# Layer 0 projection and attention: values made once, 78-row packs, first loads inside the projection, 512-wide value products

## The chip, the core and the metric

The program runs on one NeuronCore of a Trainium2 chip. Its engines work side by side: TensorE (PE) multiplies matrices, VectorE (DVE) and ScalarE (ACT) work on elements, GpSimd (POOL) too, and SyncE (SP) issues the transfers (DMAs) between HBM and the on-chip memory SBUF. PE writes to the accumulation memory PSUM. The engines are ordered by semaphores alone. The metric is the device time of one execution, in microseconds, lower is better. The kernel before takes 1454.33 us (median of 3 runs, 1447.15 to 1459.47).

## What is computed

Two transformer layers on 2048 tokens of width 128 (2 batches of 1024), each an attention and a mixture of experts, with a layer norm after each of the four parts. The change touches only the first attention, which has 16 heads of width 8 and scores made of distances instead of a softmax:

```python
qh = (q @ Wq).reshape(Bq, Sq, H, D).transpose(0, 2, 1, 3)
kh = (q @ Wk).reshape(Bq, Sq, H, D).transpose(0, 2, 1, 3)
vh = (q @ Wv).reshape(Bq, Sq, H, D).transpose(0, 2, 1, 3)
q_norm = jnp.sum(qh * qh, axis=-1, keepdims=True)
k_norm = jnp.sum(kh * kh, axis=-1, keepdims=True)
qk = jnp.einsum('bhsd,bhtd->bhst', qh, kh)
dist = jnp.maximum(q_norm - 2.0 * qk + jnp.swapaxes(k_norm, -2, -1), 0.0)
scores = jnp.exp(-gamma[None, :, None, None] * SCALE * dist)
mask = jnp.triu(jnp.ones((Sq, Sq), dtype=bool), k=1)
scores = jnp.where(mask, scores, 0.0)
out = jnp.einsum('bhst,bhtd->bhsd', scores, vh)
out = out.transpose(0, 2, 1, 3).reshape(Bq, Sq, H * D)
return out @ Wo
```

## The kernel before

Everything lies transposed: channels or keys on the partitions, tokens along the free axis. A stage is a block; all engines meet at a barrier at its end. The first blocks are these.

**First loads** (L1989). SP loads X (the input, 1 MB) and four small constants, and the block ends when they have landed.

**Projection** (`project_l0`). SP loads Wq, Wk and Hs. Then, for four groups g of 512 tokens, PE makes the queries and keys (L138, L139), ACT, DVE and POOL split each into three bf16 parts, and PE sums the squares of each head (L149), which are split too. SP stores each part to HBM (L122: three DMAs for the queries, five for the keys; L125 and L126: the norms), ten DMAs to a group. The block ends when all 40 have landed, because the attention reads them back in another order, across the groups.

**Attention** (`attention_l0`). An iteration `it` is one batch and four heads, so there are 8. For each, SP loads a pack into one of two slots: QP and KP hold 72 rows of products of parts (three parts by three parts by eight channels), and rows of norms and ones, so that one bf16 product over the partitions gives the distance. The norm rows stand at 72 and at 96, so the slots have 128 rows, whose upper half is first filled by memsets (L238: DVE fills slot 0, POOL slot 1), and SP waits for them before it loads (`slot_set`). The load is ten DMAs (L254 to L259): eight of the pack, X of the batch again (XB), and the value weights of the four heads, spread to 32 columns a head (WV).

The 1024 by 1024 upper triangle of a head is cut into 5 tiles T (TILES0), four 1024 columns wide and the last 512, so an iteration has 20 steps (T, head). Each step goes PE score products into one of three PSUM buffers `ring` (L318), ACT exp into PR (L389), DVE clamp in place (L415), POOL mask of the diagonal blocks (L291), PE value products into the PSUM buffer OUT (L338). An iteration begins with one step more: the values of its four heads (L308), which pass through `ring` too and are copied by ACT to V (L380). PE's order is fixed in the code: it runs the scores LAG = 2 tiles ahead of the value products, and puts one quarter (256 columns) of the value products of a tile behind each score step (`weigh`). The four heads of a product write 32 output rows each, at partitions 0, 32, 64 and 96. The first `weigh` of an iteration waits until DVE has copied OUT of the iteration before (`copy_out`, L420), which DVE does behind its clamps of T = 1. SP loads the pack of `it` when ACT has read all steps of `it - 2` (`ring_read`), then carries the output of `it - 2` to OC by four DMAs (L267).

After the block, the layer norm of this part begins (L501 to L541), and from there on the program is the same before and after.

Of the kernel before, what the change touches and what calls it, by code (L numbers as in the profile page):

```python
# [28 lines left out]
P = 128  # L29
# [57 lines left out]
def project_l0(nc, X, wq, wk, headsel, QS, KS, QN, KN):  # L87
# [5 lines left out]
    with ExitStack() as ctx:  # L93
# [6 lines left out]
        part = sb("p0_part", [P, 2, NPART, TOK], BF16)  # L100
        nrest = sb("p0_nrest", [2 * ROWS, TOK], F32)
        npart = sb("p0_npart", [2 * ROWS, NPART, TOK], BF16)
        psQ, psK, psN = ([pb(f"p0_{n}{s}") for s in range(2)] for n in ("psQ", "psK", "psN"))
        (loaded, proj_ready, squared, k2_done, norm_ready, part1, rest_done, part2, part3, norm_step, norm3, stored) = (
            sem(f"p0_{n}") for n in ("loaded", "proj_ready", "squared", "k2_done", "norm_ready", "part1", "rest_done",
                                     "part2", "part3", "norm_step", "norm3", "stored"))
# [4 lines left out]
        with nc.Block() as block:  # L111
            @block.sync
            def _(sp):
                sp.dma_start(Wq[:], wq).then_inc(loaded, 16)
                sp.dma_start(Wk[:], wk).then_inc(loaded, 16)
                sp.dma_start(Hs[:], headsel).then_inc(loaded, 16)
                for g in range(NG):
                    for m, (dst, copies) in enumerate(((QS, NPART), (KS, NPART + 2))):
                        for i, written in enumerate((part1, part2, part3)):
                            sp.wait_ge(written, g * 2 + m + 1)  # L120
                            for at in range(i, copies, NPART):
                                sp.dma_start(dst[:, at, :, grp(g)], part[:, m, i, grp(g)]).then_inc(stored, 16)  # L122
                    sp.wait_ge(norm_step, g * 3 + 3)
                    sp.wait_ge(norm3, g + 1)
                    sp.dma_start(QN[:, :, grp(g)], npart[0:H, :, grp(g)]).then_inc(stored, 16)  # L125
                    sp.dma_start(KN[:, :, grp(g)], npart[ROWS:ROWS + H, :, grp(g)]).then_inc(stored, 16)  # L126
                sp.wait_ge(stored, NG * (NPART + NPART + 2 + 2) * 16)

            @block.tensor
            def _(pe):  # L130
                pe.wait_ge(loaded, 48)

                def project(g):
                    if g >= 2:
# [71 lines left out]
def attention_l0(nc, x_dram, wv, gamma, QS, KS, QN, KN, OC, kept, load_ahead):  # L206

    NT = len(TILES0)
    RING, LAG = 3, 2
    STEPS = 1 + NT * HQ  # L210
    LOADS = (3 + 3 + 2 + 2) * 16
    assert STEPS % RING == 0
    with ExitStack() as ctx:
        sb, pb, sem = sbuf(nc, ctx), psum(nc, ctx), Sems(nc, ctx)
        QP = [sb(f"a0_QP{s}", [P, HQ, S], BF16) for s in range(2)]
        KP = [sb(f"a0_KP{s}", [P, HQ, S], BF16) for s in range(2)]
        XB = [sb(f"a0_XB{s}", [P, S], F32) for s in range(2)]
        WV = [sb(f"a0_WV{s}", [P, P], F32) for s in range(2)]
        V = [sb(f"a0_V{s}", [P, S], F32) for s in range(2)]
        PR = [sb(f"a0_PR{T}", [P, HQ, S], F32) for T in range(NT)]  # L220
        OALL = sb("a0_OALL", [P, NIT, S], F32)
        gam, ng, lo, hi = (sb(f"a0_{n}", [P, H], F32) for n in ("gam", "ng", "lo", "hi"))
        ring = [pb(f"a0_ring{r}", S) for r in range(RING)]
        OUT = pb("a0_OUT", S)
        pack_loaded = [sem(f"pack_loaded{s}") for s in range(2)]
        slot_set = [sem(f"slot_set{s}") for s in range(2)]
        gamma_loaded, gamma_ready = sem("gamma_loaded"), sem("gamma_ready")
        ring_filled, ring_read, clamped, masked, pv_done, out_read = (
            sem(n) for n in ("ring_filled", "ring_read", "clamped", "masked", "pv_done", "out_read"))


        def set_slot(eng, nc_eng, s):

            for n, (rows, value) in enumerate(((QP[s][64:96], 0.0), (QP[s][96:P], BF16_ONES),
                                               (KP[s][64:96], BF16_ONES), (KP[s][96:P], 0.0))):
                if n:
# [1870 lines left out]
```

## Time and profile before

| | |
|---|---|
| median of 3 runs | 1454.33 us |
| the profiled execution | 1455.11 us |
| its span on the core | 1453.4 us |
| PE busy | 1298.2 us (89%) |
| DVE busy | 1123.5 us (77%) |
| ACT busy | 908.7 us (63%) |
| POOL busy | 482.4 us (33%) |
| first matmul of the program | at 9.80 us |
| first exp of the attention | at 69.73 us |
| last copy of OUT in the attention | at 261.66 us |

The time of an execution is its span and about 2 us around it. A busy share is an average over all stages, and PE's counts matmuls that overlap, so a stage is read from its own stretch of the trace. In a timeline row the first number is the start, the second the time from the first instruction's start to the last one's end, then come engine, line, operation, what it writes and reads, the number of instructions, and in brackets how long the engine had been idle and what ended that. "SPq" is SP's DMA queue; its time is that of the issue, not of the transfer. f32 products come as two matmuls each.

### The profile page before, as it was taken

To read this page: it belongs to the slowest core of one execution; us is meant where nothing else is said; L and a number is where in the kernel's file an instruction comes from. 1 tells how busy PE (TensorE), PEld (TensorE's weight loads), DVE (VectorE), ACT (ScalarE), POOL (GpSimd) and SP (SyncE) were. 2 spreads that over 40 slices of the span, in tenths; PEclk is the share of its full clock that TensorE was granted. 3 is DMA by queue.
4 is the path that set the end of the run, shared out by engine and by line. 5 is a ranking of instruction groups with operands and counts; after the bars stand their busy time and mean duration, and the time that the engine had idled before them with its cause. 6 is when DMAs were issued, how large, how long until landed. Compare 5 with 4: busy or idle time off the path is not lost. (4 is left out here: it accounts for less than half of the span.)

```text
span 1453.4 us, 23547 instructions
## 1 busy us (share of the span) xinstructions
PE 1298.2 (89%) x7982; PEld 740.8 (51%) x7982; DVE 1123.5 (77%) x1729; ACT 908.7 (63%) x1509; POOL 482.4 (33%) x992
## 2 busy tenths in 40 slices
PE   4189898717999999999979999999999999999998
PEld 1133333415877777777743222232222327877776
DVE  4266767385999999999947888888898836688886
ACT  3188888203555555555534488878888865767774
POOL 4254545102434434434324342244224422121310
PEclk8599999957999999999998899999999998999999
DMA  4523321006566666666334475443442201021200
GB/s 133 132 56 82 81 81 31 7 0 134 132 144 151 153 144 154 149 145 155 81 120 118 103 171 135 125 102 92 109 113 66 60 5 60 28 91 73 87 30 30
DMA packets 72014, 140.46 MB, mean 97 GB/s; under 512 B 13243, under 2 KB 45436, under 8 KB 64988
## 3 DMA queue, kind: packets, MB, share of 16 engines
q1 hardware_dynamic: 70752, 138.01, 38.0%
q8 instruction: 60, 0.98, 0.3%
q10 hardware_dynamic: 1152, 1.05, 0.2%
q14 instruction: 50, 0.41, 0.1%
HBM read 121.42 MB, written 16.29 MB: 95 GB/s over the span
## 5 line engine op out<-in xcount | busy, mean ns | idle before, releaser
L1592 ACT ACTIVATE a_PR<-n1a_C 128x512 f32<-128x512 f32 x576 | 299.7, 602 | 80.6 <-PE n1a_C L1498 80.6
L1607 DVE CUSTOM_DVE_ANT_0 OC_last<-a_mring,a_COR 128x1024 bf16<-128x1024 f32 x256 | 302.7, 1218 | 44.6 <-PE a_mring L1465 44.2
L1435 POOL TENSOR_SCALAR_AFFINE_SELECT a_PR<-a_PR 128x128 f32<-128x128 f32 x512 | 136.6, 299 | 251.4 <-ACT a_PR L1592 250.8
L871 ACT ACTIVATE e_HH<-e_H 128x512 fp32r<-128x512 f32 x184 | 116.5, 633 | 162.5 <-DVE e_H L919 162.5
L1498 PE MATMUL n1a_C<-a_QP,a_KP 74*128 74x512 bf16 (+3 forms) x768 | 177.0, 333 | 6.2 <-ACT a_PR L1592 3.3
L415 DVE TENSOR_SCALAR a_PR<-a_PR,a_lo,a_hi 128x1024 f32<-128x1024 f32 (+1 forms) x160 | 122.2, 775 | 77.6 <-ACT a_PR L389 75.0
L389 ACT ACTIVATE a_PR<-a_ring,a_ng 128x1024 f32<-128x1024 f32 (+1 forms) x160 | 155.1, 1034 | 14.8 <-PE a_ring L318 14.1
L1517 PE MATMUL n1a_C<-a_PR,a_V 128*9 128x512 f32 (+3 forms) x1536 | 152.2, 492 | 0.0
L890 DVE TENSOR_TENSOR e_HL<-e_H,e_HH 128x512 fp32r<-128x512 f32 x138 | 140.7, 1019 | 13.3
L1498 PEld LDWEIGHTS n1a_C<-a_QP,a_KP 74*128 74x128 bf16 x768 | 57.1, 98 | 161.8 <-ACT a_PR L1592 120.4
L813 POOL TENSOR_TENSOR e_HL<-e_H,e_HH 128x512 fp32r<-128x512 f32 x46 | 78.8, 1714 | 182.6 <-ACT e_HH L871 182.6
L1886 DVE TENSOR_TENSOR e_HL<-e_GL,e_HH 128x512 fp32r<-128x512 f32 x144 | 108.6, 758 | 38.0 <-ACT e_HH L1854 34.3
L291 POOL TENSOR_SCALAR_AFFINE_SELECT a_PR<-a_PR 128x128 f32<-128x128 f32 x256 | 98.6, 411 | 111.1 <-DVE a_PR L415 111.1
L1847 ACT ACTIVATE e_GL<-e_psF,e_BF 128x512 f32<-128x512 f32 x144 | 99.3, 690 | 53.6 <-PE e_psF L1805 52.7
L919 DVE TENSOR_TENSOR e_H<-e_T,e_ROUTE 128x512 f32<-128x512 f32 x176 | 122.2, 694 | 1.5
L913 DVE TENSOR_TENSOR e_T<-e_SG,e_psU 128x512 f32<-128x512 f32 x176 | 119.6, 679 | 1.2 <-PE e_psU L829 1.1
L864 ACT ACTIVATE e_SG<-e_psG 128x512 f32<-128x512 f32 x184 | 108.7, 591 | 17.4 <-PE e_psG L829 17.4
L338 PE MATMUL a_OUT<-a_PR,a_V 128*32 128x256 f32 (+1 forms) x1280 | 88.7, 371 | 10.3 <-DVE a_OALL L420 10.3
L318 PE MATMUL a_ring<-a_QP,a_KP 128*128 128x512 bf16 (+3 forms) x384 | 88.0, 331 | 9.1 <-ACT a_PR L389 8.8
L1465 PE MATMUL a_mring<-a_KM,a_QM 32*128 32x512 bf16 (+3 forms) x704 | 79.0, 327 | 5.8 <-DVE a_top L1607 2.2
L827 PE MATMUL e_psG<-e_XH,e_WH 128*128 128x512 f32 x184 | 72.7, 395 | 8.6 <-POOL e_WL L808 8.6
L838 PE MATMUL e_acc<-e_HH,e_WH 128*128 128x512 f32 x184 | 76.5, 416 | 2.5 <-POOL e_HL L813 2.2
(260 smaller groups left out, 2322.2 us busy)
## 6 DMA issues: line engine op xcount, KB each, us to landing
e_ROUTE<-routing SPq DMA_DIRECT2D x24, 704.0 KB
a_QP<-q_parts SPq DMA_DIRECT2D x72, 192.0 KB
e_RAW<-in_w_chunks SPq DMA_DIRECT2D x46, 192.0 KB, 7.4
a_QM<-q_parts SPq DMA_DIRECT2D x64, 128.0 KB, 2.8
e_GATE<-gates SPq DMA_DIRECT2D x8, 1024.0 KB, 4.7
e_ROUTE<-routing SPq DMA_DIRECT2D x8, 640.0 KB
a_KP<-k_parts SPq DMA_DIRECT2D x24, 192.0 KB
e_ROUTE<-routing SPq DMA_DIRECT2D x8, 576.0 KB
```

The source lines that it names most:

```text
L389: nc.scalar.activation(PR[T][:, j, 0:WIDTH0[T]], ring[n % RING][:, 0:WIDTH0[T]], ACT.Exp, scale=ng[:, head]).then_inc(ring_read, 1)
L415: nc.vector.tensor_scalar(p, p, lo[:, head], hi[:, head], ALU.max, ALU.min).then_inc(clamped, 1)
L864: nc.scalar.activation(SG[n % 2][:], psG[n % 2][:], ACT.Silu).then_inc(silu_done, 1)
L871: nc.scalar.activation(HH[n % NH][:], HT[n % NH][:], ACT.Copy).then_inc(high_done, 1)
L890: nc.vector.tensor_tensor(HL[n % NH][:], HT[n % NH][:], HH[n % NH][:].bitcast(F32), ALU.subtract)\
L913: nc.vector.tensor_tensor(T[n % 2][:], SG[n % 2][:], psU[n % 2][:], ALU.mult).then_inc(mul_done, 1)
L919: nc.vector.tensor_tensor(HT[n % NH][:], T[n % 2][:], ROUTE[c % NW][:, grp(g)], ALU.mult).then_inc(h_ready, 1)
L1435: last = nc.gpsimd.affine_select(out=d, in_=d, compare_op=keep, fill=0.0, base=0, pattern=[[step, P]], channel_multiplier=-step)
L1498: last = nc.tensor.matmul(ring[n % NRING][:, a - h % 2 * GW:b - h % 2 * GW], KP[s][:, j, var, kb * P:(kb + 1) * P], QP[s][:, h % 2, j, var ...
L1517: last = nc.tensor.matmul(OUT[j * HP:j * HP + VC, a:b], V[:, b0 + kb, v0:v0 + VC], PR[:, g % NPR, j, a:b], start=(T == 0), stop=(T == NT - ...
L1592: nc.scalar.activation(PR[:, g % NPR, j, :], ring[n % NRING][:], ACT.Exp).then_inc(s_read, 1)
L1607: nc.vector.tensor_tensor_reduce(out=junk[:, i % 2, :], in0=mring[k % 2][:], in1=COR[:, c:c + S], scale=1.0, scalar=-3.0e38, op0=ALU.mult, ...
```

## The change

- The first block is gone. SP issues Wq, the first 512 tokens of X, Wk and Hs at the start of the projection, then the rest of X, the constants, the value weights in their own layout, gamma, and the rows of ones.
- QP and KP have 78 rows: the ones are loaded by four DMAs, the norms stand right behind the 72 rows of products, and the eight memsets are gone. One memset of OUT takes their place, since the value products now write 8 of each 32 rows.
- In the projection SP stores groups 0 and 1 (batch 0), waits for these 20 stores and issues the pack of `it = 0`. The stores of groups 2 and 3 are issued in the attention, behind the pack of `it = 1`. Batch 1's packs wait for them.
- The values of all 16 heads are made once, at the attention's start, by 8 products a batch, from X as it lies in SBUF. An iteration has 20 steps and loads eight DMAs.
- A value product is up to 512 wide, two to a tile, behind the second and the fourth score step. Its output is 8 rows a head.
- OALL holds two iterations in place of eight. From the third on, DVE's copy of OUT waits for the DMAs that read the buffer two iterations before.
- The hardware loops over iterations are written out.

The core of the diff:

```diff
+    def load_ahead(self, sp, wv, gamma, ones):
+
+        sp.dma_start(self.WV[:], wv).then_inc(self.ahead_loaded, 16)
+        sp.dma_start(self.gam[:], gamma.partition_broadcast(P)).then_inc(self.ahead_loaded, 16)
+        for s in range(2):
+            for rows in (self.QP[s][PAIRS + 3:PAIRS + 6], self.KP[s][PAIRS:PAIRS + 3]):
+                sp.dma_start(rows.rearrange("p j t -> p (j t)"), ones[0, 0:HQ * S].partition_broadcast(3)).then_inc(self.ones_loaded, 16)
+    def store_part(self, sp, g, m, i):
+
+        at = slice(g * GW, (g + 1) * GW)
+        dst, copies = ((self.QS, NPART), (self.KS, NPART + 2))[m]
+        for copy in range(i, copies, NPART):
+            sp.dma_start(dst[:, copy, :, at], self.part[:, m, i, at]).then_inc(self.stored[g // 2], 16)
...
@@ project_l0, sync @@
-                sp.dma_start(Wq[:], wq).then_inc(loaded, 16)
-                sp.dma_start(Wk[:], wk).then_inc(loaded, 16)
-                sp.dma_start(Hs[:], headsel).then_inc(loaded, 16)
-                for g in range(NG):
...
-                sp.wait_ge(stored, NG * (NPART + NPART + 2 + 2) * 16)
+                sp.dma_start(Wq[:], a["wq0"]).then_inc(loaded, 16)
+                sp.dma_start(X[:, grp(0)], a["xT"][:, grp(0)]).then_inc(loaded, 16)
+                sp.dma_start(Wk[:], a["wk0"]).then_inc(loaded, 16)
+                sp.dma_start(Hs[:], a["head_sum"]).then_inc(loaded, 16)
+                sp.dma_start(X[:, GW:], a["xT"][:, GW:]).then_inc(rest_loaded, 16)
+                for n, tile in consts.items():
+                    sp.dma_start(tile[:], a[n]).then_inc(consts_loaded, 16)
+                shared.load_ahead(sp, a["wv0"], a["gamma"], a["ones16"])
+                for g in range(2):
...
+                sp.wait_ge(consts_loaded, len(consts) * 16)
+                sp.wait_ge(shared.stored[0], shared.STORES)
+                shared.load(sp, 0)
@@ attention_l0 @@
-    STEPS = 1 + NT * HQ
+    STEPS = NT * HQ
...
+                shared.load(sp, 1)
+                for g in range(2, NG):
+                    for m in range(2):
+                        for i in range(NPART):
+                            shared.store_part(sp, g, m, i)
+                    shared.store_norms(sp, g)
+                load_ahead(sp)
+                for it in range(2, NIT):
+                    sp.wait_ge(ring_read, step(it - 1, 0, 0))
+                    if it == NQUAD:
+                        sp.wait_ge(shared.stored[1], shared.STORES)
+                    shared.load(sp, it)
+                    keep(it - 2)
...
+                def values(b):
+
+                    for kb in range(KB):
+                        at = b * S + kb * P
+                        last = nc.tensor.matmul(ring[b][:, kb * P:(kb + 1) * P], X[:, at:at + P], WV[:], start=True, stop=True)
+                    last.then_inc(ring_filled, 1)
...
-                                rows = slice(j * HP, (j + 1) * HP)
-                                last = nc.tensor.matmul(OUT[rows, a:b], V[s][:, kb * P + j * HP:kb * P + (j + 1) * HP],
-                                                        PR[T][:, j, c0 + a:c0 + b], start=(T == 0 and a % GW == 0),
+                                v0 = (q * HQ + j) * HD
+                                last = nc.tensor.matmul(OUT[j * HP:j * HP + HD, a:e], V[:, b * KB + kb, v0:v0 + HD],
+                                                        PR[T][:, j, c0 + a:c0 + e], start=(T == 0), stop=(T == NT - 1),
...
+                            half = {1: 0, 3: 1}.get(j) if T else {2: 0, 3: 1}.get(j)
+                            if half is not None and half <= (WIDTH0[T] - 1) // GW:
+                                weigh(it, T, half)
@@ attention_l0, vector @@
+                    if it >= 2:
+                        dve.wait_ge(kept[it % 2], it // 2 * HQ * 16)
+                    nc.vector.tensor_copy(OALL[:, it % 2, :], OUT[:]).then_inc(out_read, 1)
```

Two places of the order. First PE in iteration 0, from the last two steps of T = 2 to the first of T = 3, where the scores run ahead into iteration 1 (slots 0 and 1 are the last digits of QP and KP). Before:

```order
L318 MATMUL a0_ring1<-a0_QP0,a0_KP0 128x512 [waits ring_read]
L338 MATMUL a0_OUT<-a0_PR2,a0_V0 32x256 x4
L318 MATMUL a0_ring2<-a0_QP0,a0_KP0 128x512 [waits ring_read]
L338 MATMUL a0_OUT<-a0_PR2,a0_V0 32x256 x4
L308 MATMUL a0_ring0<-a0_WV1,a0_XB1 128x128 [waits ring_read,pack_loaded1]
L308 MATMUL a0_ring0<-a0_WV1,a0_XB1 128x128 x7
L318 MATMUL a0_ring1<-a0_QP1,a0_KP1 128x512 [waits ring_read]
L318 MATMUL a0_ring1<-a0_QP1,a0_KP1 128x512
L338 MATMUL a0_OUT<-a0_PR3,a0_V0 32x256 [waits masked]
L338 MATMUL a0_OUT<-a0_PR3,a0_V0 32x256 x3
```

After, the same place:

```order
L345 MATMUL a0_ring2<-a0_QP0,a0_KP0 128x512 [waits ring_read]
L345 MATMUL a0_ring0<-a0_QP0,a0_KP0 128x512 [waits ring_read]
L364 MATMUL a0_OUT<-a0_PR2,a0_V 8x256 x8
L345 MATMUL a0_ring1<-a0_QP1,a0_KP1 128x512 [waits ring_read,pack_loaded1]
L345 MATMUL a0_ring1<-a0_QP1,a0_KP1 128x512
L345 MATMUL a0_ring2<-a0_QP1,a0_KP1 128x512 [waits ring_read]
L345 MATMUL a0_ring2<-a0_QP1,a0_KP1 128x512
L364 MATMUL a0_OUT<-a0_PR3,a0_V 8x512 [waits masked]
L364 MATMUL a0_OUT<-a0_PR3,a0_V 8x512 x3
```

The values (L308) are gone from between the iterations, and two score steps stand together where one value product stood between them.

Second, SP from its last stores of the projection's block to the pack of `it = 0`. Before:

```order
L125 DMA q0_norm_parts<-p0_npart 48x1x512 [waits p0_norm3,p0_norm_step]
L126 DMA k0_norm_parts<-p0_npart 48x1x512
L111 UNCONDITIONAL_BRANCH [waits p0_stored]
L242 UNCONDITIONAL_BRANCH [waits barrier_Pool_Activation_PE_DVE_SP_release]
L244 DMA a0_gam<-in_gamma 128x16
L565 DMA WOT0<-in_wo0 128x128
L254 DMA a0_QP0<-q0_parts 24x4x1024 [waits slot_set0]
L255 DMA a0_KP0<-k0_parts 24x4x1024
```

After, from the last stores of group 1 to the pack of `it = 1`; the stores of groups 2 and 3 follow it:

```order
L124 DMA k0_norm_parts<-p0_npart 48x1x512
L133 DMA a0_QP0<-q0_parts 24x4x1024 [waits p0_stored0,p0_consts_loaded]
L134 DMA a0_KP0<-k0_parts 24x4x1024
...
L136 DMA a0_KP0<-k0_norm_parts 3x4x1024
L164 UNCONDITIONAL_BRANCH
L289 UNCONDITIONAL_BRANCH [waits barrier_Pool_Activation_PE_DVE_SP_release]
L133 DMA a0_QP1<-q0_parts 24x4x1024
```

The first pack now stands ahead of the block's end and behind 20 stores; before it stood behind 40 stores, the barrier and the memsets.

## Rows read from the trace of the kernel before

**Rows 1.** Windows: length, PE, PEld, DVE, ACT, POOL busy (count), PEclk, DMA share, GB/s.

```profile
165.88:189.92 24.04, 21.78 (x225) 8.85 (x224) 16.33 (x21) 20.33 (x23) 12.23 (x32) 1.00 0.31 82
103.00:105.00 2.00, 2.00 (x18) 0.58 (x9) 1.60 (x3) 0.39 (x1) 1.72 (x4) 0.50 0.24 33
105.00:107.00 2.00, 2.00 (x21) 0.78 (x19) 0.45 (x1) 1.11 (x1) 0.73 (x3) 0.69 0.26 41
```

**Rows 2.** Timeline of ACT in iteration 4, and its first exp of the stage.

```profile
69.73 17.80 ACT L389 ACTIVATE a_PR<-a_ring,a_ng 128x1024 f32<-128x1024 f32 x18
...
177.98 1.11 ACT L389 ACTIVATE a_PR<-a_ring,a_ng 128x1024 f32<-128x1024 f32 x1 [0.82 <-PE a_ring L318]
179.59 5.73 ACT L389 ACTIVATE a_PR<-a_ring,a_ng 128x1024 f32<-128x1024 f32 x6 [0.50 <-PE a_ring L318]
...
189.00 1.02 ACT L380 ACTIVATE a_V<-a_ring 128x1024 f32<-128x1024 f32 x1 [1.89 <-PE a_ring L308]
```

**Rows 3.** Timeline of PE in the same iteration.

```profile
162.78 2.05 PE L308 MATMUL a_ring<-a_WV,a_XB 128*128 128x128 f32 x16
164.66 0.59 PE L318 MATMUL a_ring<-a_QP,a_KP 128*128 128x512 bf16 x2
...
171.31 1.48 PE L318 MATMUL a_ring<-a_QP,a_KP 128*128 128x512 bf16 x9
...
176.26 1.07 PE L338 MATMUL a_OUT<-a_PR,a_V 128*32 128x256 f32 x16 [1.46 <-DVE a_OALL L420]
...
177.81 1.07 PE L338 MATMUL a_OUT<-a_PR,a_V 128*32 128x256 f32 x16
178.81 0.61 PE L318 MATMUL a_ring<-a_QP,a_KP 128*128 128x512 bf16 x3
179.35 0.64 PE L338 MATMUL a_OUT<-a_PR,a_V 128*32 128x256 f32 x8
179.92 0.61 PE L318 MATMUL a_ring<-a_QP,a_KP 128*128 128x512 bf16 x3
```

**Rows 4.** Timeline of PE in the second layer's attention, whose value products are 512 wide.

```profile
941.68 1.05 PE L1517 MATMUL n1a_C<-a_PR,a_V 128*9 128x512 f32 x8
942.66 0.82 PE L1498 MATMUL n1a_C<-a_QP,a_KP 74*128 74x512 bf16 x3
```

**Rows 5.** Timeline of SP's queue to the first pack.

```profile
0.82 0.39 SPq L1992 DMA_DIRECT2D X<-in_xT  x1
...
7.88 0.42 SPq L116 DMA_DIRECT2D p_Hs<-in_head_sum  x1
...
27.63 0.59 SPq L126 DMA_DIRECT2D k_norm_parts<-p_npart  x1
...
40.61 0.59 SPq L126 DMA_DIRECT2D k_norm_parts<-p_npart  x1
43.17 0.33 SPq L244 DMA_DIRECT2D a_gam<-in_gamma  x1
...
52.21 0.93 SPq L254 DMA_DIRECT2D a_QP<-q_parts  x1
...
57.73 0.28 SPq L257 DMA_DIRECT2D a_KP<-k_norm_parts  x1
```

**Rows 6.** DMA issues: times, KB each, median us from issue to landing.

```profile
X<-in_xT SPq DMA_DIRECT2D x1, 1024.0 KB, 4.8
```

**Rows 7.** Timeline of PE, POOL and DVE at the stages' borders.

```profile
9.80 2.07 PE L138 MATMUL p_psQ<-X,p_Wq 128*128 128x512 f32 x2 [9.80 <-DMA p_Hs<-in_head_sum]
...
32.23 1.14 POOL L188 TENSOR_TENSOR p_npart<-p_nrest,p_npart 64x512 bf16<-64x512 f32 x1 [0.36 <-DVE p_npart L178]
...
64.93 3.78 PE L308 MATMUL a_ring<-a_WV,a_XB 128*128 128x128 f32 x16 [34.93 <-DMA a_WV<-in_wv]
68.50 1.12 PE L318 MATMUL a_ring<-a_QP,a_KP 128*128 128x512 bf16 x4
...
261.66 1.23 DVE L420 COPY a_OALL<-a_OUT 128x1024 f32<-128x1024 f32 x1 [1.86 <-PE a_OUT L338]
```

More of the change, by code:

```diff
@@ L227, in attention_l0 @@
[L227 to L236, printed above, removed]
-                    eng.wait_ge(slot_set[s], n)
-                nc_eng.memset(rows.bitcast(F32), value).then_inc(slot_set[s], 1)
-            eng.wait_ge(slot_set[s], 4)
+        gamma_ready, out_clear, ring_filled, ring_read, clamped, masked, pv_done, out_read = (
+            sem(n) for n in ("gamma_ready", "out_clear", "ring_filled", "ring_read", "clamped", "masked", "pv_done", "out_read"))
@@ L346, in pair @@
+                    if half == (WIDTH0[T] - 1) // GW:
+                        last.then_inc(pv_done, 1)
+                pe.wait_ge(shared.ahead_loaded, 32)
+                for b in range(B):
+                    values(b)
+                pe.wait_ge(shared.ones_loaded, 64)
+                for T in range(LAG):
+                    for j in range(HQ):
+                        scores(0, T, j)
+                pe.wait_ge(out_clear, 1)
+                for it in range(NIT):
                     for T in range(NT):
-                        ahead = T + LAG < NT or not last_pair
@@ L348, in pair @@
-                        if T + LAG == NT and ahead:
-                            values(it + 1, k + s, 1 - s)
                         for j in range(HQ):
                             if T + LAG < NT:
-                                scores(it, T + LAG, j, s)
-                            elif ahead:
-                                scores(it + 1, T + LAG - NT, j, 1 - s)
-                            for quarter in {0: (), 1: (), 2: (0, 1), 3: (2, 3)}[j] if T == 0 else (j,):
-                                if quarter <= (WIDTH0[T] - 1) // (GW // 2):
-                                    weigh(it, T, s, quarter)
@@ L360, in _ @@
[L360 to L370 removed]
+                                scores(it, T + LAG, j)
+                            elif it + 1 < NIT:
+                                scores(it + 1, T + LAG - NT, j)
@@ L392, in _ @@
-                pair(0, 0, 0, True)
-                pair(1, 1, 1, False)
-                with act.Fori(1, NIT // 2) as k:
-                    for s in range(2):
-                        pair(k * 2 + s, (k % 2) * 2 + s, s, False)
+                            n, head = step(it, T, j), it % NQUAD * HQ + j
+                            act.wait_ge(ring_filled, n + 1)
+                            if j == 0 and it:
+                                act.wait_ge(pv_done, (it - 1) * NT + T + 1)
+                            nc.scalar.activation(PR[T][:, j, 0:WIDTH0[T]], ring[n % RING][:, 0:WIDTH0[T]],
+                                                 ACT.Exp, scale=ng[:, head:head + 1]).then_inc(ring_read, 1)
```

237 lines of the change are left out of this document (95 added, 142 removed).

## Prediction

> **What bounds the kernel now.** I read the timelines of SP, PE and ACT from the start to the end of the first attention, and windows of one iteration. The stages behind it are not touched, so every microsecond by which that attention ends earlier is one off the total.
>
> Up to the first score product everything waits for SP and for transfers. The program's first matmul starts at 9.80, when Hs has landed [rows 7], though SP was free to load it from 0.82 on. SP issues the last of the projection's 40 stores at 40.61 and the next block begins at 43.17 [rows 5], while the projection's last computation ended at 33.37 [rows 7]. The memsets hold the first pack load back to 52.21 [rows 5]. PE starts the values at 64.93, the scores at 68.50 [rows 7], ACT its exps at 69.73 [rows 2].
>
> In the steady iterations PE sets the pace. A period is 24.04, of which PE works 21.78 and ACT 20.33 [rows 1]. PE's 2.26 idle are 1.46 for DVE's copy of OUT [rows 3] and two short waits for `ring`. ACT waits 0.82 and 0.50 behind that same copy, and 1.89 for the values [rows 2]. DVE (16.33) and POOL (12.23) [rows 1] have slack. The last copy of OUT ends at 262.89 [rows 7].
>
> **The start.** (a) First matmul. SP's issues are about 0.45 apart, so Hs, now fourth, is issued at about 2.2. Before it took 1.92 from issue to the matmul [rows 5, 7], giving 4.1. Ahead of it stands a quarter of X; all of X took 4.8 to land [rows 6], so the quarter adds some tenths. I take 4.5, a gain of 5.3 (bounds 4 and 6). The other three quarters of X, issued at 2.7, should land by about 7.5; the second group's projection wants them 3.6 after the first matmul.
>
> (b) Stores. From the first matmul to the issue of group 1's last store were 17.83 (9.80 to 27.63) [rows 5, 7]. SP now has 11 more loads to issue first, 5 us, over at about 8.3; the stores of group 0 then still wait for POOL's third part, so I add nothing. That issue stands at 22.3. A last store's issue to the next block took 2.56 (40.61 to 43.17) [rows 5], landing and barrier, of which some 2.2 are landing. The first pack's issue starts at 24.6 where it started at 52.21. Its eight issues take 5.8 (52.21 to past 57.73) [rows 5], so the block ends at 30.8. The computation of groups 2 and 3 does not hold it: it ended at 33.37 [rows 7] and moves up by 5.3, to 28.1. The remaining 20 stores, with 0.65 each (12.98 for twenty, 27.63 to 40.61 [rows 5]), go behind the pack of iteration 1; batch 1's packs are not wanted for another 60 us, and the pack of iteration 1 itself is issued from 31 on and wanted near 52.
>
> (c) Values and first exp. PE begins at 31. Sixteen value instructions took 3.57 at the start (64.93 to 68.50) [rows 7] and 1.88 in the loop (162.78 to 164.66) [rows 3]. Two batches are 32. With the clock up after the first batch that is 5.5, wholly slow 7.1; I take 5.5. The first pack, 8 to 9 us after 24.6, is there by then. ACT copies the second batch's values (1.02 [rows 2]) and starts its exps at about 37.6. Before: 69.73 [rows 2]. The start gains **32.1** (bounds 28 and 34). DVE's memset of OUT lies under the values; without that cover it would cost about as much as a copy, 1.2.
>
> **The period.** (d) Values gone: 1.88 of PE. (e) Fewer alternations. Two 256-wide quarters in a row take 1.00 (177.81 to 178.81), one between scores 0.57 (179.35 to 179.92) [rows 3]: a quarter streams in 0.43 and each change of kind costs 0.14. A score step between products takes 0.54 (178.81 to 179.35), three in a row 1.48 or 0.47 each [rows 3], so 0.07 more. An iteration loses seven alternations (two in T = 1, 2 and 3, one in T = 4; T = 0 keeps its two): 7 x 0.21 = 1.5. The 512-wide product with few output rows is in this trace: eight instructions of 128x512 with 9 columns go in 0.98 (941.68 to 942.66), beside scores of 74 rows [rows 4], what 2 x 0.43 + 0.14 gives. So neither 8 output rows nor 78 rows cost or gain anything. The Trainium skill (TensorEngine Tiling, Key Properties) says that changing the tiling mode drains TensorE. It states no price; the 0.21 is the trace's.
>
> PE's work becomes 21.78 - 1.88 - 1.5 = 18.4. ACT's is 16 exps at 0.99 (18 in 17.80 [rows 2]) and four half-wide ones at 0.6 by my estimate (0.5 to 0.7, half the width at somewhat over half the time), 18.2. The two engines are now level, and the copy of OUT stays where it is: DVE copies it behind the clamps of T = 1, PE's first value product waits behind three score steps. PE alone gives 18.4 + 1.46 = 19.9, ACT with its 0.82 and 0.50 19.5. As both run through three buffers with products in lumps of 0.98, and ACT outruns PE in the half-wide tile, they add some waits. Laying the steps out one behind the other from one copy to the next, with the durations above, I get 20.4 to 20.8. I take **20.6**, a gain of 3.44.
>
> (f) Seven periods lie between the first exps of iterations 0 and 7: 24.1. In the last there are no scores ahead to interleave; its tail shrinks by about 0.6. Together **24.7** (19.9 would give 29.6, 21.8 only 16).
>
> (g) The rest: OALL's new wait needs DMAs issued more than an iteration earlier; if they were late DVE would stall, with PE behind it and ACT behind PE. A pack load is released at the end of an iteration and wanted some 20 us on, and needs 9. The written-out loops I cost at nothing: iterations 0 and 1 were written out before.
>
> **Sum.** 32.1 + 24.7 = 56.8. The profiled execution took 1455.11 with a span of 1453.4; it becomes 1398.3. It stands 0.8 above the median, so the median is 1397.5; I say **1398**.
>
> **Rivals.**
> 1. *ACT paces.* A lone exp takes 1.11 [rows 2], not 0.99. If they do not close up, ACT needs 16 x 1.11 + 2.8 + 1.3 = 21.9 a period, a gain of 2.1 in place of 3.44: 1398 + 7 x 1.3 = 1407. For it: PE no longer leaves it behind. Against: 18 in a row at 0.99.
> 2. *The clock falls at the copies.* From 103 to 107 the granted clock was 0.50 and then 0.69, right after PE had waited for a copy [rows 1]. That costs 1.0 + 0.6 us. It happened in one of seven copies, and it is in the time before. PE will idle 11% of a period in place of 9%. If it came at every copy: 6 more x 1.6, 1398 + 10 = 1408. The Trainium skill (TensorE: Matmul & The Clock Gate, A second HAM failure mode) says that frequent short idling between groups makes the clock swing. By that rule this rival comes true; the trace so far agrees once in seven.
> 3. *The start does not come forward.* If the pack load still waits for something that I take as free (20 more requests early on, X arriving late), up to 8 us of the 32 stay: 1406.
> 4. *Smoother.* The copy's wait is all that is left, period 19.9: 1393.
> 5. *Slower than before.* If the four products with 8 output rows did not run side by side in the array, a half tile would stream four times 0.86: 2.6 more for each of 9 products, 23 us a period, 1398 + 184 = 1582. It decides from 57 us over 72 products on, that is if one takes more than 1.8 in place of 0.98. Against it stands the 0.98 of [rows 4] with 9 columns.
> 6. *No change*: would need the packs to be read later than computed by 57 us; I see no path.
>
> **How the numbers follow.** My forecast (1388 to 1403) has 0.54, rival 1 0.12, rival 2 0.12, rival 3 0.08, rival 4 with a start at its better bound 0.1, slower 0.02, no change 0.02. The range reaches from rival 4 with one microsecond more at the start and in the tail each (1390, rounded out to 1386) to rivals 1 and 2 with some microseconds of (a) to (c) on top (1414). This kernel's measurement can tell about 1% from no change, that is 1440; all cases but the last two lie below: faster 0.96.
>
> **What would show it.** In the changed kernel: first matmul near 4.5; first pack issue near 24.6, barrier near 31, first exp near 37.6; half-tile products 0.98 to 1.0 apart from what follows; period between first exps 20.4 to 20.8; the copy of OUT still waited for by 1.5; granted clock 1.00 in the iterations; everything behind the attention as long as before. I am wrong if the first exp comes after 43, if the period is above 21.5, or if a later stage has grown.

## The result and the profile after

The changed kernel takes **1404.14 us** (median of 3 runs, 1402.02 to 1405.89) where the kernel before takes 1454.33: a ratio of 0.9685, with the interval 0.9643 to 0.9726. It is faster by 50.2 us. The forecast was 1398, the range 1386 to 1414. So the number was right, but two of its parts were off, and they partly cancel: the gain of the iterations and the stages behind. The experiments are about the first.

| | before | after |
|---|---|---|
| the profiled execution | 1455.11 | 1402.02 |
| its span | 1453.4 | 1400.3 |
| first matmul | 9.80 | 4.78 |
| first pack issued | 52.21 | 24.86 |
| first exp | 69.73 | 38.48 |
| seven periods, from the first exp of iteration 0 to that of iteration 7 | 168.27 | 154.76 |
| last copy of OUT begins | 261.66 | 217.24 |
| layer norm's first instruction on ACT | 266.31 | 221.88 |
| span behind that | 1187.1 | 1178.4 |

Busy times by the page: PE 1279.3 us (91%), DVE 1114.2 (80%), ACT 898.5 (64%), POOL 481.3 (34%).

**The start.** SP's queue and PE after, the places of [rows 5] and [rows 7]:

```profile
22.63 0.59 SPq L124 DMA_DIRECT2D k_norm_parts<-p_npart  x1
24.86 0.89 SPq L133 DMA_DIRECT2D a_QP<-q_parts  x1
...
30.31 0.28 SPq L136 DMA_DIRECT2D a_KP<-k_norm_parts  x1
31.12 0.77 SPq L133 DMA_DIRECT2D a_QP<-q_parts  x1
```

```profile
4.78 2.07 PE L198 MATMUL p_psQ<-X,p_Wq 128*128 128x512 f32 x2 [4.78 <-DMA p_Hs<-in_head_sum]
...
31.17 6.35 PE L333 MATMUL a_ring<-a_WV,X 128*128 128x128 f32 x32 [6.18 <-PEq L164]
```

The last store of group 1 is issued at 22.63, the pack 2.2 behind it, and the eight issues of the pack end just before the next block begins. PE then makes all values in 6.2 us, and ACT can start:

```profile
38.48 11.15 ACT L402 ACTIVATE a_PR<-a_ring,a_ng 128x1024 f32<-128x1024 f32 x11
```

**The iterations.** Windows of the first five of them, each from the first exp of one iteration to that of the next; columns as in [rows 1], the last but two is the granted clock.

```profile
38.48:58.87 20.39, 18.19 (x111) 4.88 (x112) 14.93 (x20) 18.72 (x21) 13.20 (x31) 0.83 0.44 121
58.87:79.22 20.35, 18.09 (x145) 5.28 (x144) 16.03 (x22) 18.74 (x21) 13.20 (x33) 1.00 0.25 68
79.22:101.87 22.65, 20.59 (x145) 5.40 (x144) 15.90 (x22) 18.73 (x20) 13.20 (x33) 0.85 0.23 62
101.87:125.14 23.27, 21.01 (x145) 5.58 (x144) 15.91 (x22) 18.91 (x21) 12.83 (x33) 0.85 0.22 59
125.14:147.06 21.92, 19.66 (x145) 5.35 (x144) 15.90 (x22) 18.73 (x20) 13.19 (x33) 0.92 0.24 63
```

The second is the iteration that the prediction worked out (period 20.35, PE busy 18.09, clock 1.00). Those behind it have the same 145 matmuls and the same work on ACT, but PE is busy for 1.6 to 2.9 us longer, and the granted clock is 0.85 to 0.92. The first, iteration 0, has fewer matmuls and no copy to wait for, and its clock is 0.83; the run with 128 rows below shows what that costs. The seven periods are 20.39, 20.35, 22.65, 23.27, 21.92, 22.86 and 23.32.

Inside such an iteration, windows of 2 us (same columns):

```profile
87.00:89.00 2.00, 0.82 (x4) 0.21 (x3) 1.80 (x3) 2.00 (x3) 1.85 (x5) 0.67 0.02 4
89.00:91.00 2.00, 1.51 (x8) 0.15 (x8) 2.00 (x4) 1.37 (x2) 0.87 (x2) 0.50 0.10 14
91.00:93.00 2.00, 2.00 (x11) 0.41 (x11) 0.51 (x1) 0.61 (x1) 1.64 (x5) 0.50 0.33 49
93.00:95.00 2.00, 2.00 (x13) 0.44 (x6) 0.81 (x1) 0.56 (x2) 0.54 (x2) 0.62 0.01 2
95.00:97.00 2.00, 2.00 (x17) 0.63 (x15) 0.81 (x1) 2.00 (x3) 0.03 (x1) 1.00 0.00 0
```

PE works for 0.82 of the first 2 us (it waits for ring buffers and then for the copy of OUT), the clock goes to 0.50, which is the lower of its two levels, 1.2 GHz, and PE then works without a pause at that level until about 94.5, before 2.4 GHz are granted again. The timeline of PE shows it at the first product behind each copy. First the copy without a fall, then two with:

```profile
69.14 1.04 PE L364 MATMUL a_OUT<-a_PR,a_V 128*8 128x512 f32 x8 [1.47 <-DVE a_OALL L420]
70.12 0.61 PE L345 MATMUL a_ring<-a_QP,a_KP 78*128 78x512 bf16 x3
...
89.48 1.90 PE L364 MATMUL a_OUT<-a_PR,a_V 128*8 128x512 f32 x8 [1.27 <-DVE a_OALL L420]
...
112.14 1.90 PE L364 MATMUL a_OUT<-a_PR,a_V 128*8 128x512 f32 x8 [1.47 <-DVE a_OALL L420]
113.97 1.03 PE L345 MATMUL a_ring<-a_QP,a_KP 78*128 78x512 bf16 x3
114.94 1.90 PE L364 MATMUL a_OUT<-a_PR,a_V 128*8 128x512 f32 x8
```

The wait is about the same 1.46 as before [rows 3] (1.27 at 89.48); the instructions behind it take 1.8 times as long. Six of the seven copies that PE waits for look like the later ones. ACT, which now has little slack, stands behind PE each time:

```profile
115.05 1.11 ACT L402 ACTIVATE a_PR<-a_ring,a_ng 128x1024 f32<-128x1024 f32 x1 [2.02 <-PE a_ring L345]
117.84 2.12 ACT L402 ACTIVATE a_PR<-a_ring,a_ng 128x1024 f32<-128x1024 f32 x2 [1.68 <-PE a_ring L345]
```

**The end of the stage**, DVE's last copy and ACT's first instruction of the layer norm:

```profile
217.24 1.23 DVE L420 COPY a_OALL<-a_OUT 128x1024 f32<-128x1024 f32 x1 [1.96 <-PE a_OUT L364]
```

```profile
221.88 1.28 ACT L513 ACT_TABLE_LOAD   x1 [7.17 <-PEq L288]
```

The last copy comes 44.4 us earlier than before: 31.25 from the start, 13.5 from the seven periods, 0.3 given back behind them. The two profiled executions differ by 53.1; the missing 8.7 lie in stages whose code is the same.

### The profile page after: what moved, and what is told of

It is laid out like the page before. It is cut to its first block and busy times, and to the rows that moved or that the text cites. A ratio compares the mean times of both kernels' runs of the same rounds, so it can differ in the third digit from the quotient of the medians.

```text
span 1400.3 us, 21389 instructions
## 1 busy us (share of the span) xinstructions
PE 1279.3 (91%) x7374; PEld 711.9 (51%) x7374; DVE 1114.2 (80%) x1726; ACT 898.5 (64%) x1503; POOL 481.3 (34%) x988
## 5 line engine op out<-in xcount | busy, mean ns | idle before, releaser
L1432 POOL TENSOR_SCALAR_AFFINE_SELECT a_PR<-a_PR 128x128 f32<-128x128 f32 x512 | 136.2, 296 | 250.2 <-ACT a_PR L1589 249.7
L402 ACT ACTIVATE a_PR<-a_ring,a_ng 128x1024 f32<-128x1024 f32 (+1 forms) x160 | 150.2, 1045 | 26.0 <-PE a_ring L345 26.0
L427 DVE TENSOR_SCALAR a_PR<-a_PR,a_lo,a_hi 128x1024 f32<-128x1024 f32 (+1 forms) x160 | 119.2, 763 | 56.1 <-ACT a_PR L402 55.6
L887 DVE TENSOR_TENSOR e_HL<-e_H,e_HH 128x512 fp32r<-128x512 f32 x138 | 139.4, 1010 | 13.5 <-DVE e_H L904 0.5
L323 POOL TENSOR_SCALAR_AFFINE_SELECT a_PR<-a_PR 128x128 f32<-128x128 f32 x256 | 105.3, 444 | 82.0 <-DVE a_PR L427 82.0
L861 ACT ACTIVATE e_SG<-e_psG 128x512 f32<-128x512 f32 x184 | 108.7, 591 | 23.3 <-PE e_psG L826 23.1
L364 PE MATMUL a_OUT<-a_PR,a_V 128*8 128x512 f32 (+3 forms) x768 | 84.8, 542 | 10.1 <-DVE a_OALL L420 10.1
L345 PE MATMUL a_ring<-a_QP,a_KP 78*128 78x512 bf16 (+3 forms) x384 | 86.1, 351 | 7.8 <-ACT a_PR L402 7.5
```

Of the source, the lines that this page charges most:

```text
L402: nc.scalar.activation(PR[T][:, j, 0:WIDTH0[T]], ring[n % RING][:, 0:WIDTH0[T]], ACT.Exp, scale=ng[:, head:head + 1]).then_inc(ring_read, 1)
L427: nc.vector.tensor_scalar(p, p, lo[:, head:head + 1], hi[:, head:head + 1], ALU.max, ALU.min).then_inc(clamped, 1)
L887: nc.vector.tensor_tensor(HL[n % NH][:], HT[n % NH][:], HH[n % NH][:].bitcast(F32), ALU.subtract)\
L1432: last = nc.gpsimd.affine_select(out=d, in_=d, compare_op=keep, fill=0.0, base=0, pattern=[[step, P]], channel_multiplier=-step)
```

## The experiments

Three theories of why the periods gain 13.5 in place of 24.1:

- **The wait.** PE's wait for DVE's copy is what brings the clock down. Without it there is no fall at these places.
- **The thin operands.** The wait was there before, with one fall in seven copies [rows 1, 3]. What is new are packs of 78 rows and outputs of 8 rows a head, and one or both of them make the difference.
- **The missing values.** The 1.88 us of value products between the iterations are gone, so PE works less between two waits.

"Falls" below counts, of the seven copies for which PE waits, those behind which the first value product takes 1.3 to 2 us instead of 1.04 to 1.07. "Stage end" is the start of ACT's table load. The fall in iteration 0, where PE waits for no copy, is not among the seven.

The first four runs come from one chip, the next four from a second, the last four from a third. The kernel before took 1451.75, 1450.29 and 1452.39 there (medians), so one or two microseconds between runs of different chips say nothing.

**The changed kernel again**, nothing edited.

> The changed kernel as it is, for the spread. Attention as in its first profile: first exp near 38.5, undisturbed periods 20.4, five or six copies of OUT followed by a fall of the granted clock, last copy of OUT near 218. The stages behind the attention were 8.7 us shorter than before in the first pair of profiles although their code is the same. If that is chance, they differ by some microseconds from profile to profile here, and the median lies at 1402 to 1408.

Measured: 1407.96 (ratio 0.9705, 0.9661 to 0.9749). Falls 7 of 7, seven periods 159.15, stage end 228.09. Each copy reads like this one:

```profile
92.44 1.90 PE L364 MATMUL a_OUT<-a_PR,a_V 128*8 128x512 f32 x8 [1.46 <-DVE a_OALL L420]
```

So the falls belong to the kernel, and how many there are, and what one costs, differs between executions: this profile lost 4.4 us more over the seven periods than the first, and its longest period was 24.96, 4.6 above the undisturbed 20.35.

**The copy one tile earlier**, in the changed kernel. OUT is complete soon after T = 0 of the next iteration has been clamped, so DVE can copy it there.

```diff
-                        if T == 1 and it:
+                        if T == 0 and it:
                             copy_out(it - 1)
```

> One line of the changed kernel: DVE copies OUT behind its clamps of T = 0 instead of T = 1. Theory A (PE's wait for the copy brings the clock down): the wait of 1.46 is gone, the granted clock stays 1.00, period 18.9 in all iterations, last copy near 196, total 22 us below the changed kernel, about 1382. Theory B (the clock falls because the new products fill less of the array, wait or no wait): periods 20.5 to 21.5 with falls in most iterations, total 8 to 12 below, about 1393.

Measured: **1383.07** (1374.22 to 1388.35), ratio 0.9521 (0.946 to 0.9582). No fall at the seven places, stage end 201.83. Window of one iteration, then PE and DVE at the copy:

```profile
116.91:136.27 19.36, 18.13 (x145) 5.28 (x144) 16.04 (x22) 18.59 (x20) 14.26 (x33) 1.00 0.28 72
```

```profile
102.88 1.23 DVE L420 COPY a_OALL<-a_OUT 128x1024 f32<-128x1024 f32 x1 [0.36 <-PE a_OUT L364]
```

```profile
105.74 0.61 PE L345 MATMUL a_ring<-a_QP,a_KP 78*128 78x512 bf16 x3 [0.40 <-ACT a_PR L402]
106.28 1.05 PE L364 MATMUL a_OUT<-a_PR,a_V 128*8 128x512 f32 x8
```

The copy is over at 104.1, two microseconds before PE wants OUT, and the product behind it has no wait and its full speed. PE still has its two waits of 0.40 for a ring buffer, and here they bring no fall. The undisturbed period falls by 1.0 (20.35 to 19.36; 18.9 was expected), not by the whole 1.46, and the falls at the copies are gone: together 26.3 us by the stage's end against the run above, 24.9 by the medians. The theory of the wait holds for these falls. The one in iteration 0 is still there (clock 0.83, period 20.34). The run does not say yet why the kernel before got away with the same wait.

**The same line in the kernel before.**

```diff
-                        if T == 1 and not first:
+                        if T == 0 and not first:
```

> The kernel before with the same one line. Both theories: the wait of 1.46 goes, period 24.04 to 22.5; seven times 1.5 and the one fall of 1.7, total 12 below before, about 1442.

Measured: 1442.45 (ratio 0.9933, 0.991 to 0.9957), near the expected 1442, though against the 1451.75 of its chip it gained 9.3 where 12 were expected; period 23.19 where 24.04 stood [rows 1] and 22.5 was expected, stage end 257.94, 8.4 earlier. The wait was worth 9.3 us there and 24.9 in the changed kernel. The difference is what the change made of the wait.

**Quarters again**: value products 256 wide, one quarter behind each score step, the rest as changed.

```diff
...
-                            half = {1: 0, 3: 1}.get(j) if T else {2: 0, 3: 1}.get(j)
-                            if half is not None and half <= (WIDTH0[T] - 1) // GW:
-                                weigh(it, T, half)
+                            for quarter in {0: (), 1: (), 2: (0, 1), 3: (2, 3)}[j] if T == 0 else (j,):
+                                if quarter <= (WIDTH0[T] - 1) // (GW // 2):
+                                    weigh(it, T, quarter)
```

> The changed kernel with value products 256 wide, one quarter behind each score step, as before. The alternations return: PE's work rises by 1.5, an undisturbed period is 21.6 to 21.9. Theory A in its form that PE's idle share matters: fewer falls, since PE idles less; all periods near 21.7, total within 3 us of the changed kernel. Theory B: the falls stay, periods 23 to 24, total 8 above it, about 1412.

Measured: 1402.19 (ratio 0.9658, 0.9601 to 0.9715). Periods from 21.36 to 23.35, five of them at 23.3; stage end 226.87. So falls come with the narrow products too. While the clock falls, undoing the wide products costs nothing that the times show (1402.19 beside 1407.96 and 1404.14). The one period with the clock at 1.00 is 21.77, 1.42 above the 20.35 with the halves, while a fall costs about 1.55 here and 1.6 to 4.6 there. A later run prices the width without falls.

**32 output rows**: the value products take 32 columns of V (8 of the head and the 24 behind them), packs as changed. V gets 24 columns of zeros at its end, and OUT needs no memset.

```diff
-        V = sb("a0_V", [P, B * KB, P], F32)
+        V = sb("a0_V", [P, B * KB, P + HP - HD], F32)
...
-                                last = nc.tensor.matmul(OUT[j * HP:j * HP + HD, a:e], V[:, b * KB + kb, v0:v0 + HD],
+                                last = nc.tensor.matmul(OUT[j * HP:(j + 1) * HP, a:e], V[:, b * KB + kb, v0:v0 + HP],
```

> The changed kernel with value products of 32 output rows a head, as before (24 of them hold products nobody reads). Three theories on why the granted clock now falls at six of seven copies and fell at one before. C (8 output rows): falls become rare here, periods 20.4, total 10 to 13 below the changed kernel, about 1396. R (78 rows in the scores) and V (PE has 3.4 us less work from copy to copy while the wait is as long): nothing changes here, 1405 to 1409.

Measured: 1396.64 (ratio 0.9634, 0.959 to 0.9678). Falls 4 of 7, stage end 220.40. A product takes 1.06 without a fall, 1.04 with 8 rows. The profiled execution took 1392.15, two others 1401.13 and 1402.01; its stage ended only 1.5 before that of the changed kernel's first profile, and its later stages were the shortest of all profiles. The interval of its ratio overlaps those of the two runs of the changed kernel. So this run does not show that the thin outputs bring falls.

**128 rows in the packs**: rows 64 to 127 of the four slots are zeroed by POOL at the projection's start, ones and packs are loaded over them as changed, and 50 rows stay zero. The sum over the partitions is the same.

```diff
-        self.QP = [sb(f"a0_QP{s}", [PAIRS + 6, HQ, S], BF16) for s in range(2)]
-        self.KP = [sb(f"a0_KP{s}", [PAIRS + 6, HQ, S], BF16) for s in range(2)]
+        self.QP = [sb(f"a0_QP{s}", [P, HQ, S], BF16) for s in range(2)]
+        self.KP = [sb(f"a0_KP{s}", [P, HQ, S], BF16) for s in range(2)]
...
+        sp.wait_ge(self.rows_zero, 4)
...
+                for n, t in enumerate(shared.QP + shared.KP):
+                    if n:
+                        pool.wait_ge(shared.rows_zero, n)
+                    nc.gpsimd.memset(t[64:P].bitcast(F32), 0.0).then_inc(shared.rows_zero, 1)
```

> The changed kernel with packs of 128 rows, the 50 others zero (four memsets on POOL at the start, the ones loaded behind them, which may cost the start up to 2 us). Theory R: falls become rare, periods 20.4, total 8 to 12 below the changed kernel. Theories C and V: nothing changes but the start, 1406 to 1411.

Measured: 1391.19 (ratio 0.9583, 0.9553 to 0.9612). First exp at 38.41, as changed. Falls 1 of 7, stage end 207.62. Two iterations, with and without the fall:

```profile
87.83:109.47 21.64, 19.00 (x142) 5.37 (x145) 15.91 (x22) 18.74 (x21) 13.20 (x32) 0.93 0.25 64
109.47:129.81 20.34, 17.77 (x142) 5.27 (x145) 16.02 (x22) 18.74 (x21) 13.20 (x32) 1.00 0.26 68
```

```profile
109.47 1.04 PE L371 MATMUL a_OUT<-a_PR,a_V 128*8 128x512 f32 x8 [1.46 <-DVE a_OALL L427]
```

The wait is there with its full 1.46, and in six of seven copies the clock stays up. Zero rows that add nothing to the result save 13 to 17 us. In iteration 0 the clock stays up too:

```profile
38.41:57.22 18.81, 15.25 (x109) 4.69 (x112) 14.78 (x20) 18.49 (x21) 13.93 (x31) 1.00 0.51 140
```

That is 1.6 us less than the 20.39 of the changed kernel. Until the clock falls, PE does the same in both: from 40 to 42 it is busy for 1.20 of 2 us, in front of each score step it waits 0.40 for a ring buffer, and no copy is involved. Every profile of this case repeats the difference. The nine of kernels with 78-row packs show a granted clock of 0.77 to 0.84 in iteration 0, the five with 128 rows 1.00. Of all that was tried this speaks most plainly for the packs.

**The values once more**: the changed kernel with a 21st step in each iteration, in which PE makes its batch's values again and ACT copies them to a buffer that nothing reads.

```diff
...
+                    for kb in range(KB):
+                        at = b * S + kb * P
+                        last = nc.tensor.matmul(ring[n % RING][:, kb * P:(kb + 1) * P], X[:, at:at + P], WV[:], start=True, stop=True)
...
+                    nc.scalar.activation(VX[:], ring[n % RING][:], ACT.Copy).then_inc(ring_read, 1)
```

> The changed kernel which beside all else makes a batch's values once more per iteration, as one more step of the ring, and never reads them. That prices the values: 1.88 of PE, 1.02 of ACT and its wait, undisturbed period 22.6 to 23.2 for 20.4. Theory V: PE works as long between the copies as the kernel before nearly did, falls become rare, first exp of iteration 0 to that of iteration 7 takes 160, total near 1408. Theories C and R: falls stay, period 24.5 to 25.5, that stretch takes 172, total near 1422.

Measured: 1424.77 (ratio 0.9814, 0.9787 to 0.984). Falls 7 of 7, seven periods 171.0, stage end 242.13. PE's added work does not keep the clock up: the third theory falls. The run also prices the values: 11.9 us over seven periods beside the changed kernel's repetition, which also fell seven times, that is 1.7 a period, close to the 1.88 of step (d). The falls were shorter in this profile, though: periods with a clock of 0.92 to 0.93 took 21.93 there and 24.29 here, 2.4 apart. So the price lies between 1.7 and 2.4, ACT's copy and the ring step included.

**All 40 stores ahead of the first pack**, with the early copy, so that no fall blurs it.

```diff
-                for g in range(2):
+                for g in range(NG):
...
```

> The early-copy kernel (so that no fall of the clock blurs it) with all 40 stores ahead of the first pack. Prices the split of the stores: twenty issues at 0.65 are 13.0 us, first pack issue from 24.9 to 37.9, first exp from 38.5 to 50 or 51 (the pack's landing, under cover of the values so far, may add up to 3), total 12 to 15 above the early-copy kernel, 1395 to 1398. If the start hung on something else, less than 5.

Measured: 1396.05 (ratio 0.9623, 0.9601 to 0.9644), 13.0 above the early copy alone, or 14.4 if each is taken from the kernel before on its own chip. First pack and first exp are 11.6 and 10.9 later, stage end 213.45 (+11.6):

```profile
36.56 0.89 SPq L133 DMA_DIRECT2D a_QP<-q_parts  x1
```

So splitting the stores is worth 11 to 14 us. This profile also has one more fall: in iteration 5 (period 20.40 for 19.36, clock 0.92) behind two waits of 0.40, with the copy long done:

```profile
154.07 0.61 PE L340 MATMUL a_ring<-a_QP,a_KP 78*128 78x512 bf16 x3 [0.40 <-ACT a_PR L397]
155.07 0.61 PE L340 MATMUL a_ring<-a_QP,a_KP 78*128 78x512 bf16 x3 [0.40 <-ACT a_PR L397]
155.61 1.80 PE L359 MATMUL a_OUT<-a_PR,a_V 128*8 128x512 f32 x8
```

So the earlier copy makes falls rare with 78-row packs, and doesn't exclude them.

**Early copy and quarters.** The edit for the quarters is the one above.

> The early-copy kernel with value products 256 wide, one behind each score step. Prices the 512-wide products where no clock fall blurs them. By the sum of the prediction they save 1.4 to 1.5 of PE an iteration: period from 19.36 to 20.2 to 20.8, last copy 7 to 10 later, total 7 to 10 above the early-copy kernel. If the width is worth nothing even there (ACT paces at 19.36): under 2 above it.

Measured: 1395.51 (ratio 0.9622, 0.956 to 0.9684). No fall after iteration 0:

```profile
101.51:122.43 20.92, 19.57 (x212) 6.20 (x210) 15.95 (x22) 19.42 (x20) 14.10 (x32) 1.00 0.25 67
```

PE is busy for 19.57 beside 18.13 with the halves, the period is 20.92 beside 19.36. The 512-wide products are worth 1.56 a period where no fall blurs it, 11.0 by the stage's end (212.82 for 201.83) and 12.4 in all; 7 to 10 were expected.

**Early copy and 128 rows.**

> The early-copy kernel with packs of 128 rows, 50 of them zero. If a fall needs both, the wait for the copy and the thin packs, there is nothing left to save: period 19.36, total within 3 us of the early-copy kernel (1380 to 1386). If the thin packs cost something beside the falls, 4 or more below it.

Measured: 1383.3 (ratio 0.9511, 0.944 to 0.9583), period 19.39, stage end 201.34: the same as the early copy with 78 rows, as far as the times show. Thin packs stream neither faster nor slower. They cost through the clock, and with the early copy that is little: iteration 0 takes 18.81 here at clock 1.00 and 20.34 there at 0.83, and the first exp came 0.9 later here.

**128 rows and 32 output rows**, the late copy as changed; both edits from above.

> The changed kernel (late copy) with both undone, 128-row packs and 32 output rows. The 128-row packs alone left one fall of seven (1391), the 32 rows alone four (1397). If both act on the same thing, no fall is left, every period 20.4, total 1388 to 1391. If the 32 rows only looked better by chance, as many falls as with the packs alone, one or two, 1390 to 1393.

Measured: 1389.71 (ratio 0.9594, 0.953 to 0.9658). Falls 0 of 7 with the full wait at each, stage end 207.35:

```profile
88.11:108.58 20.47, 18.21 (x145) 5.74 (x146) 16.00 (x22) 18.80 (x21) 13.26 (x32) 1.00 0.25 67
```

**Only the thin packs, in the kernel before**: 78 rows, ones by DMA, no memsets.

```diff
...
-        QP = [sb(f"a0_QP{s}", [P, HQ, S], BF16) for s in range(2)]
-        KP = [sb(f"a0_KP{s}", [P, HQ, S], BF16) for s in range(2)]
+        QP = [sb(f"a0_QP{s}", [PAIRS + 6, HQ, S], BF16) for s in range(2)]
+        KP = [sb(f"a0_KP{s}", [PAIRS + 6, HQ, S], BF16) for s in range(2)]
...
```

> The kernel before with one part of the change: 78-row packs, the ones loaded, no memsets. The start gains the 8.3 us from the slot's memsets (first pack issue 52.2 to about 45.5, since four small loads come first; first exp 69.7 to 62 or 63). If the thin packs bring the falls, they come here too, at four to seven of the seven copies for one before, 1.7 to 2.3 each: iterations 0 to 7 take 176 to 180 for 168.3, total 0 to 4 above or below before. If they don't: 168.3, total 7 to 8 below before.

Measured: 1449.17 (ratio 0.9992, 0.9957 to 1.0027), no change that the measurement can tell. The first exp came at 62.30, 7.4 earlier than before, and the stage ended at 268.03, 1.7 later. The loop took back 9 us. There were three falls at the copies by the count used here, and a fourth that began one microsecond behind the copy's first product, at 197 (period 25.63); four to seven were expected. One more is in iteration 0, where PE waits for no copy:

```profile
62.30:84.66 22.36, 20.19 (x148) 6.27 (x148) 14.56 (x19) 18.83 (x21) 11.79 (x30) 0.77 0.07 17
```

So thin packs bring falls in the older loop too (0.77 in this window, where the kernel before has 1.00 in iteration 0), at some copies and not at others. This part of the change, taken alone, would have been measured as worth nothing: its 7.4 us at the start went into the clock.

The runs on the falls side by side:

| packs | output rows a head | copy | falls of 7 | clock in iteration 0 | stage end | median |
|---|---|---|---|---|---|---|
| 78 | 8 | late (as changed) | 6 | 0.83 | 221.88 | 1404.14 |
| 78 | 8 | late, again | 7 | 0.83 | 228.09 | 1407.96 |
| 78 | 32 | late | 4 | 0.77 | 220.40 | 1396.64 |
| 128 | 8 | late | 1 | 1.00 | 207.62 | 1391.19 |
| 128 | 32 | late | 0 | 1.00 | 207.35 | 1389.71 |
| 78 | 8 | early | 0 | 0.83 | 201.83 | 1383.07 |
| 128 | 8 | early | 0 | 1.00 | 201.34 | 1383.30 |

The number of falls is that of one profiled execution for each row. The medians, over three or four executions, stand in nearly the same order. The kernel with values made once more, also 78 and 8 and late, fell at 7 of 7 on the chip of the third and fourth rows.

## Why the prediction was right, point by point

- **(a) First matmul**: said 4.5, is 4.78. The gain is 5.0 in place of 5.3.
- **(b) Stores and pack**: group 1's last store said at 22.3, is 22.63; pack at 24.6, is 24.86; block's end at 30.8, next issue at 31.12. Right, and the run with all stores first confirms the mechanism with 11 to 14 us.
- **(c) Values and first exp**: values said 5.5, are 6.2 (31.17 to 37.35). The clock was 0.50 for the first 3.13 us and 0.64 for the rest; the forecast had it up for the second batch. First exp said 37.6, is 38.48. The start gained 31.25 of the forecast 32.1.
- **(d), (e) The undisturbed period**: said 20.6 (20.4 to 20.8) with PE's work at 18.4; it is 20.35 with 18.09. The values were worth 1.7 to 2.4 (said 1.88), the alternations 1.56 (said 1.5). The Trainium skill's sentence that a change of the tiling mode drains TensorE (TensorEngine Tiling, Key Properties) fits that last number, 1.56 us a period for seven alternations less in the run with early copy and quarters; the page has no price of its own.
- **(f) Seven periods and tail**: this is the step that failed. Said 24.7, is 13.2 (13.5 less 0.3). The undisturbed period itself would have brought 168.3 - 7 x 20.35 = 25.8; the falls at copies in five of the seven periods took 12.3 of it, and a sixth such fall lies in the tail. The step also took all seven periods as alike. Iteration 0 waits for no copy and would have taken 18.8 at full clock, as with 128 rows; its own fall made it 20.39, so that this slip does not show in the sum.
- **Rival 2** named this mechanism and its place. Its chance of 0.12 was too small, and its price of 1.6 a fall too low: the five falls cost 1.6 to 3.0, mean 2.5. The 1.6 counted only the time in which PE worked at the lower level in one place of the trace, where ACT had slack behind PE; now ACT has 18.7 us of work in a period of 20.35 and loses what PE loses. For the chance I had put the one fall in seven down to luck and let the new idle share of 11% change little. The runs show that what changed was something else, the operands, of which step (e) had said that neither 8 output rows nor 78 rows "cost or gain anything". As to how long an instruction streams that was right (0.97 to 0.98, 52.27 to 53.24 after), as to the clock it was wrong. What the Trainium skill reports of one kernel, that frequent short idling between groups makes the clock swing (TensorE: Matmul & The Clock Gate, A second HAM failure mode), was the better guide here: this trace agrees with it at six of seven copies, and the run with 128 and 32 rows, the same idling and no fall, shows that idling alone does not decide.
- **Rivals 1, 3, 4, 5, 6** did not come. In the changed kernel 11 exps take 11.15, so they close up. The start came. With the wait the period is 20.35, not 19.9; even without it it is 19.36, 1.2 above PE's work. Eight output rows stream like 32 (1.04 and 1.06 a product). The packs are read sooner.
- **(g) The rest**: said nothing, and in the two profiles the span behind the stage is 8.7 shorter. From the layer norm's first instruction that computes on ACT to the last squares of the last norm the same code took 1175.0 in the profile before, 1166.4 after, and between 1158.0 and 1172.4 in the twelve other profiles. So most of it can be chance, the profile of before being the longest of the fourteen. All of it need not be: the three profiles with the older attention ahead are the three longest (1175.0, 1172.4, 1171.1; the others reach 1170.7 at most), which is open.

In sum: the attention ended 12.4 us later than forecast (0.9 from the start, 10.6 from the periods, 0.9 from the tail), and 8.7 us came from stages that vary by 17 between profiles. The difference, 3.7, is what separates the profiled 1402.0 from the forecast 1398.3. The number was close for reasons that the prediction had only half, and for the rest by luck.

**A better kernel.** The changed kernel with the one-line earlier copy takes 1383.07, 68.7 less than the kernel before on the same chip and 24.9 less than the changed kernel there.

**What stays open.** The runs show that thinner packs make falls behind unchanged waits more frequent. They do not show why, nor why some copies of one kernel bring a fall and others do not. That thinner outputs add to it is not shown: with 78-row packs the counts are 6, 7 and 7 against 4, with 128-row packs 1 against 0, from one profile each, and the times of the two runs with 128 rows overlap (1387.42 to 1394.17 and 1388.19 to 1395.30).

## What to carry to other kernels

Copy a shared accumulator out as soon as it is complete, not just ahead of its next use: here a TensorE wait of 1.5 us cost 1.6 to 4.6 us more through the clock. Waits of 0.40 in front of every score step were enough in iteration 0. After an edit that makes TensorE's operands smaller, read the granted clock iteration by iteration even where every instruction takes as long as before; rows and columns that hold nothing can be cheaper to keep. Where a forecast counts periods, give each period its chance of a fall, and price the fall by what both engines lose.

## What was unexpected of the hardware

- Zero rows kept the clock up: with 50 of them added to the packs, and the same waits of 1.46, the falls went from 6 or 7 of 7 copies to 1, and the time from 1404 to 1408 down to 1391. With early copies the same rows were worth nothing that the times show (1383.3 and 1383.07), and 1.5 us in iteration 0.
- The same waits of 0.40 in iteration 0 brought the granted clock to 0.50 from about 43.3 on with 78-row packs and left it at 1.00 with 128 rows.
- A value product that took 1.04 took 1.72 to 1.90 in a fall, the score steps with it. In the windows after, the clock fell between 87 and 88 and was back between 94 and 95.
- The later stages, the same code in all profiles, took from 1158 to 1175 us. A difference of 8 us between two single profiles, in stages that an edit doesn't touch, is no evidence of a gain here.
